# Layer-norm statistics taken one stage earlier, output stored in pieces, and query lengths by column tiles, in a 12-stage decoder kernel

## The reference

```python
def _layernorm(x, axis=-1, eps=1e-05):
    m = jnp.mean(x, axis=axis, keepdims=True)
    v = jnp.var(x, axis=axis, keepdims=True)
    return (x - m) / jnp.sqrt(v + eps)
...
# layer 1, cross-attention, for each of 16 heads with D = 128
q = rmsnorm(q, gq); k = rmsnorm(k, gk)      # x * rsqrt(mean(x^2) + eps) * g
```

## Time and profile before

| | |
|---|---|
| median of three runs | 1930.0 us (1928.4 to 1930.96) |
| profiled execution | 1931.94 us, its span 1930.2 us |
| busy, share of the span | PE 1709.8 us (89%), DVE 1174.4 (61%), ACT 927.5 (48%), POOL 442.2 (23%) |
| weight loads of PE | 1334.9 us (69%) |
| mean granted TensorE clock | 0.951 of full speed |
| DMA | 77.87 MB, 40 GB/s over the span |
| one row load of 129 KB (`xnT<-rows_sent`, 23 of them) | 2.0 us from issue to landing (median) |

### The profile page before, as it was taken

One profiled execution on the slowest core, in us unless ns is written; L12 is line 12 of the kernel. 1 busy time (PEld: TensorE's weight loads), 2 busy tenths in 40 slices (PEclk: granted clock), 3 DMA queues, 4 the chain that ended last, 5 costly groups with the idle time before them and its releaser, 6 DMA issues. The chain is left out here.

```text
span 1930.2 us, 37486 instructions
## 1 busy us (share of the span) xinstructions
PE 1709.8 (89%) x13958; PEld 1334.9 (69%) x13958; DVE 1174.4 (61%) x2339; ACT 927.5 (48%) x1966; POOL 442.2 (23%) x497
## 2 busy tenths in 40 slices
PE   7978846789999889977878879999999988999898
PEld 4767724569999745643667747777777776888666
DVE  3676687655555612226654577888888865666632
ACT  2445565245555511112254356766666744555532
POOL 1020011033333032221300133545454531000200
PEclk9999977899999989998979889999999999999999
DMA  2020001200010182221000100101010103110000
GB/s 100 3 90 3 4 29 50 93 17 26 25 29 28 53 326 42 45 52 43 14 2 3 42 9 26 33 25 33 25 33 25 33 9 127 36 33 24 1 1 23
DMA packets 27105, 77.87 MB, mean 40 GB/s; under 512 B 2928, under 2 KB 14832, under 8 KB 24560
## 3 DMA queue, kind: packets, MB, share of 16 engines
q1 hardware_dynamic: 22912, 71.17, 10.9%
q0 software_dynamic: 4080, 5.13, 1.7%
HBM read 63.01 MB, written 13.28 MB: 40 GB/s over the span
## 5 line engine op out<-in xcount | busy, mean ns | idle before, releaser
L2473 DVE SCALAR_TENSOR_TENSOR arena<-bank,arena 128x508 f32<-128x508 f32 (+2 forms) x204 | 151.6, 743 | 29.9 <-ACT arena L2469 17.9
L217 PE MATMUL bank<-const 128*128 128x256 f32 (+1 forms) x228 | 95.8, 535 | 33.7 <-PEq L65 33.7
L2599 PE MATMUL bank<-L3a_wo,L3a_y_gated 128*128 128x256 f32 x512 | 124.0, 386 | 0.0
L2827 DVE TENSOR_TENSOR L3a_decays<-L3a_decays,L3a_cb_masked 128x512 f32<-128x512 f32 x128 | 95.0, 804 | 43.9 <-ACT L3a_decays L2711 43.9
L2711 ACT ACTIVATE L3a_decays<-bank 128x512 f32<-128x512 f32 x128 | 66.1, 604 | 98.2 <-PE bank L2573 98.2
L2626 PE MATMUL bank<-L3a_xnT_high,L3a_w_high 128*128 128x512 f32 x256 | 106.3, 415 | 1.5 <-ACT L3a_decays L2711 1.5
L2599 PEld LDWEIGHTS bank<-L3a_wo,L3a_y_gated 128*128 128x128 f32 x512 | 92.4, 190 | 17.6 <-issue 7.3
L2626 PE MATMUL bank<-L3a_xnT_high,L3a_w_low 128*128 128x512 f32 x256 | 100.5, 393 | 0.0
L2626 PE MATMUL bank<-L3a_xnT_low,L3a_w_high 128*128 128x512 f32 x256 | 100.4, 392 | 0.0
L1885 PE MATMUL bank<-L1f_experts,xnT 128*128 x184 | 84.5, 602 | 1.0 <-DVE xnT L1987 0.7
L2922 POOL TENSOR_TENSOR arena<-arena 128x1024 f32<-128x1024 f32 x32 | 81.1, 2533 | 14.8 <-ACT arena L2718 14.8
(11 more groups left out here) (593 smaller groups left out, 4706.1 us busy)
## 6 DMA issues: line engine op xcount, KB each, us to landing
arena<-in_L3p SPq DMA_DIRECT2D x32, 388.0 KB, 3.0
L1f_experts<-in_L1f SPq DMA_DIRECT2D x8, 1536.0 KB, 19.3
arena<-in_L1x SPq DMA_DIRECT2D x18, 384.0 KB, 3.1
arena<-in_L3x SPq DMA_DIRECT2D x18, 384.0 KB, 3.0
arena<-in_L0f SPq DMA_DIRECT2D x1, 4224.0 KB, 13.6
arena<-in_L3f SPq DMA_DIRECT2D x1, 4055.0 KB, 12.6
rows_sent<-L1a_blank SPq DMA_DIRECT2D x1, 2967.0 KB, 13.9
xnT<-rows_sent SPq DMA_DIRECT2D x23, 129.0 KB, 2.0
```

The lines of the kernel that those rows point to most:

```text
L217: self.nc.tensor.matmul(self.k.ps[bank][:, 0:width], self.k.ident, self.k.const[:, 0:width], start=True, stop=True)
L2473: return nc.vector.scalar_tensor_tensor(dst[:, :, d:], psum[:, :, 0:P - d], wcol, dst[:, :, d:], ALU.mult, ALU.add)
L2599: mm = nc.tensor.matmul(ps[g // 2][:, (g % 2) * C:(g % 2 + 1) * C], yg[:, o, g * P:(g + 1) * P], wo[:, o, :], start=False, stop=False, ski ...
L2827: nc.vector.tensor_tensor(d, d, cbm[:, 4 * half:4 * half + 4, :].rearrange("p b t -> p (b t)"), ALU.mult).then_inc(S["dec_ready"], 1)
```

## The change

- `Norm(measured=True)`, in 11 of the 12 stages (not L0a): no `bn_stats`. DVE runs eight `bn_aggr`, ACT one square root for all eight batches, DVE one reciprocal and one bias. PE keeps the two opening unread matmuls, and has one more ahead of batches 1 and 2 only, not ahead of 3, 5, 6, 7.
- `measure` runs `bn_stats` in the stage before, on DVE behind each addition, after a wait for that addition's own semaphore. In L0f and L1a batches 0 to 5 are measured ahead of the last but one addition, in L3a all eight behind the last addition. L1f fetches x with two DMAs of 512 KB, and measures four batches behind each.
- `WideHeads.add` waits for each half of the last projection instead of for the whole.
- ACT preloads the table of the square root at the end of each stage from L0a to L3x.
- The output is stored from L3f by four DMAs of 256 KB, each behind its addition. "end" only clears semaphores.
- L1x: the lengths of a head come from four matmuls with ones (128x32) as weights and 256 squared columns moving, each to its own 32 partitions of bank 7; they stand ahead of the scores. DVE copies the 128x256 result to SBUF, PE transposes it in two pieces behind the scores, and DVE picks 8 columns of that.

```diff
+        if self.measured:
+            for b in range(NB):
                 nc.vector.bn_aggr(k.ln_mv[:, b, :], k.ln_stats[:, b, :]).then_inc(self.s_mv, 1)
+            self.scales(dve, 0)
+            for b in self.BY_DVE:
+                normed(b)
...
-                if j and self.busy:
+                if self.busy and b in ((1, 2) if self.measured else (1, 2, 3, 5, 6, 7)):
                     self.idle(pe, 1, C)
...
+def measure(k, dve, sem, added, batches):
+    dve.wait_ge(sem, added)
+    for b in batches:
+        k.nc.vector.bn_stats(k.ln_stats[:, b, :], k.x[:, b, :])
...
-    def add(self, dve):
+    def add(self, dve, N):
         x = self.k.x
         for n in range(4):
+            dve.wait_ge(self.s_y, 2 * N - 1 + n // 2)
             self.nc.vector.tensor_tensor(x[:, 2 * n:2 * n + 2, :], x[:, 2 * n:2 * n + 2, :],
-                                         self.k.ps[n][:, :].rearrange("p (b n) -> p b n", b=2), ALU.add)
+                                         self.k.ps[n][:, :].rearrange("p (b n) -> p b n", b=2),
+                                         ALU.add).then_inc(self.s_x, 1)
+            measure(self.k, dve, self.s_x, n + 1, (2 * n, 2 * n + 1))
...
+                nc.scalar.preload_act_table(ACT.Sqrt)
...
                 for n in (NB - 2, NB - 1):
+                    measure(k, dve, s_x, n, range(0, n) if n == NB - 2 else (n - 1,))
                     added(n)
+                measure(k, dve, s_x, NB, (NB - 1,))
...
                 sp.wait_ge(s_added, NT * 16)
-                sp.dma_start(x[:, :, :], k.sums[0:TOK, :].rearrange("(p b) c -> p b c", b=NB)).then_inc(s_fetched, 16)
-                sp.wait_ge(s_fetched, 16)
+                for n in range(2):
+                    bs = slice(4 * n, 4 * n + 4)
+                    sp.dma_start(x[:, bs, :], k.sums[0:TOK, :].rearrange("(p b) c -> p b c", b=NB)[:, bs, :]).then_inc(
+                        s_fetched[n], 16)
...
+                    measure(k, dve, S["x_added"], NB, range(NB))
...
+                        tr.free(pe, j, ("n", 0))
+                        pe.wait_ge(s_sq, j * 2 + 2)
+                        for r in range(4):
+                            mm = nc.tensor.matmul(tr.bank(("n", 0))[32 * r:32 * r + 32, 0:C], k.c["ones"][:, 0:32],
+                                                  sq[:, r * C:(r + 1) * C], start=True, stop=True)
+                        mm.then_inc(s_len, 1)
                     if back:
...
                         a.scores(pe, j, "", 1 - s)
                     if now:
-                        tr.free(pe, j, ("n", 0))
-                        pe.wait_ge(s_sq, j * 2 + 2)
-                        for b in range(NB):
-                            mm = nc.tensor.matmul(tr.bank(("n", 0))[:, b:b + 1], sq[:, b * P:(b + 1) * P],
-                                                  k.c["ones"][:, 0:1], start=True, stop=True)
+                        pe.wait_ge(s_lenc, j + 1)
+                        for n in range(2):
+                            mm = nc.tensor.transpose(tr.bank(("n", 0))[:, C + n * P:C + (n + 1) * P],
+                                                     lengths[:, n * P:(n + 1) * P], k.ident)
                         mm.then_inc(s_n, 1)
...
+                    if now:
+                        dve.wait_ge(s_len, j + 1)
+                        since(dve, s_n, j)
+                        nc.vector.tensor_copy(lengths[:, :], tr.bank(("n", 0))[:, 0:C]).then_inc(s_lenc, 1)
...
+                for n in range(4):
+                    sp.wait_ge(s_x, n + 1)
+                    sp.dma_start(k.out[:, 2 * n:2 * n + 2, :], x[:, 2 * n:2 * n + 2, :]).then_inc(s_out, 16)
+                sp.wait_ge(s_out, 64)
...
-                    sp.dma_start(out, k.x[:, :, :]).then_inc(s_out, 16)
                     for s in [*k.used, k.s_sent, k.s_added]:
                         sp.sem_clear(s)
-                    sp.wait_ge(s_out, 16)
-                    sp.sem_clear(s_out)
```

More of the change, by code:

```diff
@@ L123, with __init__ @@
     BY_ACT, BY_DVE = (0, 1, 2, 6), (3, 4, 5, 7)
-    def __init__(self, k, st, halves=None, turned=True, busy=True):
+    def __init__(self, k, st, halves=None, turned=True, busy=True, measured=True):
         self.k, self.nc, self.halves, self.turned, self.busy = k, k.nc, halves, turned, busy
+        self.measured = measured
         self.s_stats, self.s_mv, self.s_std = st.sem("ln_stats"), st.sem("ln_mean_var"), st.sem("ln_std")
@@ L199, in scalar @@
         for b in self.BY_ACT:
-            if b == 2:
+            if b == 2 and not self.measured:
                 std(1)
-            if b == 6:
+            if b == 6 and not self.measured:
                 act.wait_ge(self.s_nbias, 2)
@@ L599, in dve @@
             own = x[:, 2 * n:2 * n + 2, :].rearrange("p b n -> p (b n)")
-            self.nc.vector.tensor_tensor(own, own, self.k.ps[4 + n if self.turned else n][:, :], ALU.add)
+            self.nc.vector.tensor_tensor(own, own, self.k.ps[4 + n if self.turned else n][:, :],
+                                         ALU.add).then_inc(self.s_x, 1)
+            measure(self.k, dve, self.s_x, n + 1, (2 * n, 2 * n + 1))
 def clear(nc, t, sem):
@@ L1511, in _ @@
                         add(b - 2)
-                add(NB - 2)
-                add(NB - 1)
+                for b in (NB - 2, NB - 1):
+                    measure(k, dve, s_x, b, range(0, b) if b == NB - 2 else (b - 1,))
+                    add(b)
+                measure(k, dve, s_x, NB, (NB - 1,))
 def l1_xattn(k):
@@ L1552, in l1_xattn @@
         s_wh, s_qw = st.sem("w_high"), st.sem("q_w_ready")
+        s_len, s_lenc = st.sem("lengths_psum"), st.sem("lengths_copied")
         s_lns, s_rn = st.sem("log_ready"), st.sem("rnorm_ready")
@@ L2001, in _ @@
                                                 ALU.mult).then_inc(s_yc, 1)
+                for n in range(2):
+                    measure(k, dve, s_fetched[n], 16, range(4 * n, 4 * n + 4))
 def l2_attn(k):
@@ L3413, in program @@
     k = K()
-    k.nc, k.dram, k.parts, k.width = nc, dram, parts, width
+    k.nc, k.dram, k.parts, k.width, k.out = nc, dram, parts, width, out
     with ExitStack() as ctx:
```

90 lines of the change are left out of this document (55 added, 35 removed).

## The result

The changed kernel takes 1913.1 us (median of four, 1910.8 to 1915.5) against 1929.2 for the kernel before on the same chip: ratio 0.991, 95% interval 0.9893 to 0.9927, so 16 us faster by the medians and 17 by the ratio.

What follows compares the result with a forecast made beforehand. The openings were taken as one chain with PE bounding its later part, the L1x loop as PE's. Openings -23.1, moved statistics +13.9, clock +2.4, tail +1.0, L1x -14.3: -20.1 us, giving 1910 us, range 1903 to 1923.

Steps and rivals of the forecast that it cites:

- (c): Openings: transposes don't hold the clock, ten blocks start at half speed, 1.64 us each, 1926 us; chance 0.06.
- (d): L1x lengths: four column groups run one after another, +0.25 us a head, 1928 us, no change; chance 0.06.
- (e): L1x lengths: groups run one by one and each pass awaits its weight load, 1940 us; chance 0.05.
- The step from 3.32 to 2.1 for the first transpose: Full-clock openings: the earlier square root brings PE's first transpose to 2.1 us after the barrier instead of 3.32.
- The four unread matmuls at 1.76: Stage openings: removing four unread matmuls between transposes, 0.44 us each, shortens the chain by 1.76 us.
- The 1.1 for two close additions in L2x: L2x's end: two additions stand close together and the queue behind them is late, costing 1.1 us.
- the 1.75 forecast: L1f's fetch: x's second half lands one issue (0.32) later and four statistics follow, costing 1.75 us.
- None to four can fall, I take two: Clock in the four fast stages' openings: longer barrier gaps, 1.2 us per fall, 2.4 us taken (0 to 4.8).
- Each of the fast stages would lose 0.57: Openings: if the square root's table load stayed at the barrier, each full-clock stage would lose 0.57 us.
- Rival (b): Openings: the preload doesn't take away the table load at the stage's start, 2.3 us, 1912 us; chance 0.08.
- 1.06: L1x loop: PE saves 1.06 us a head with the new lengths; 14 heads less 0.5 make 14.3 us.
- Rival (a): L1x loop: not PE's alone, PE waits for q, half of the 14.3 us is kept, 1917 us; chance 0.15.

Runs made afterwards that it cites:

- experiment 8: The changed kernel without the preloads of the square root's table at the stages' ends; ratio to the kernel before 0.991.
- experiment 5: The changed kernel with the statistics back in every stage's opening, unread matmuls ahead of batches 1 and 2 only; ratio to the kernel before 0.9873.
- experiment 2: The changed kernel with L1x's eight length matmuls of before in place of the length tiles; ratio to the kernel before 0.9945.
- experiment 4: The changed kernel with the wait for the stored quarters moved behind the 44 semaphore clears; ratio to the kernel before 0.9894.
- experiment 7: The changed kernel without any unread matmul between transposes in the measured stages, the two opening ones kept; ratio to the kernel before 0.9894.
- 9: The changed kernel once more, unaltered (the repeat); ratio to the kernel before 0.9907.
- experiment 10: The changed kernel with all six unread matmuls between the transposes put back; ratio to the kernel before 0.9984.
- experiment 1: The kernel before with only the L1x length tiles of the change; ratio to the kernel before 0.9943.
- experiment 3: The kernel before without the unread matmuls ahead of batches 3, 5, 6, 7, statistics left in place; ratio to the kernel before 0.9919.
- 6: The changed kernel with statistics moved for L0f only, stores awaited behind clears shared by four engines; ratio to the kernel before 0.9879.
- 11: The changed kernel with statistics moved for L0f only and clears shared by four engines, timed again; 1904.3 us, ratio to the kernel before 0.9854.

## Why the prediction was right, and where it wasn't

**The time.** 1910 was forecast, 1913.1 measured. The forecast mechanism held in nearly every place, and rivals (c), (d), (e) are refuted by the traces. Two terms were mis-sized, L1x by 5 us and the other blocks, which I had at nothing, by 3 the other way. That the second made up for more than half of the first is luck: it hangs on where the clock stood in these two profiles.

**Openings.** The step from 3.32 to 2.1 for the first transpose: 2.21. The four unread matmuls at 1.76: 1.74. So 2.9 in L2f and L3a: 2.91 and 2.92, with the block at 5.77 after the barrier (5.7 was said). L1a, L1f and L2a at 1.76: 1.72, 1.74, 1.74. L0f 1.7: 1.92. L3x 0.9: 1.22. In L2x it was 2.49, since ACT's first normed batch started 1.2 after the start of the square root and not 0.78, as in L2f; I had 0.75 to 0.91 for all. L3f gave only 0.73: I counted it with the stages at half clock whose opening stays as long as it was, but its clock came back among the transposes, later after the barrier than before, so that the transposes ran at half clock too. In L1x 1.9 was forecast; 0.52 is in this profile and 2.22 in the repeat, as the clock fell or held. But in the repeat it fell 0.9 us into the block, which took 255.1 us instead of 252.8, so that most of the 2.22 was lost again there.

**Ends of stages.** 0.78 was said for L0a, L0x, L2a and L2f: 0.78, 0.80, 0.79 in L0a, L0x and L2f. The 1.1 for two close additions in L2x is wrong: it has 0.79. L2a has 1.12 in its place, but for another reason: its additions are 1.73 apart, and DVE waits 0.97 at that barrier where it waits 0.64 elsewhere, so DVE isn't what the barrier waits for. In experiment 8, without preloads, L2a's end is 0.34 shorter; in experiment 5, with the preload and without the moved statistics, it is 1.27, as before. So the preload has a part in it, how stays open. L0f and L1a 0.5: 0.44, 0.45. L1x and L3x 2.0: 1.74 and 1.69. L3a 2.9: 2.74, the long row of this timeline (DVE):

```profile
1566.16 3.23 DVE L2948 SCALAR_TENSOR_TENSOR x<-bank,L3a_rms,x 128x256 f32<-128x256 f32 x8
1569.42 2.71 DVE L264 BATCH_NORM_STATS2 ln_stats<-x 128x6 f32<-128x256 f32 x8
```

In L1f from the fetch to the barrier 7.1 us pass instead of 5.5, so 1.6 for the 1.75 forecast, but not as I had it. The rows of the changed kernel:

```profile
854.11 0.79 SPq L1867 DMA_DIRECT2D x<-rows_added  x2
```

```profile
857.96 2.72 DVE L264 BATCH_NORM_STATS2 ln_stats<-x 128x6 f32<-128x256 f32 x8 [9.24 <-DMA x<-rows_added]
```

The first half lands 3.85 after the issue, earlier than I assumed, and the second before the first's statistics are through; all eight `bn_stats` are exposed in one row, none hides under the second half. The wrong mechanism came out at the right size, which is luck.

**The clock.** "None to four can fall, I take two": one of the four (L0x) fell in this profile. Over the seven profiles with moved statistics (after, 2, 4, 7, 8, 9, 10) L0x, L2x, L2f and L3a make 28 openings, of which 15 fell, 2.1 in each. Over the six with their statistics at home (before, 1, 3, 5, 6, 11) none of 24 fell. What differs is PE's idle time at the barrier, 2.15 us there (2.5 in L2x) and 1.36 here. Neither the unread matmuls nor the preload make the difference: openings fell in experiment 10 with all of the first and in experiment 8 without the second. L1x, L1f and L3f, whose clock was at 1.00 before the barrier in every profile too, give further gaps:

| PE's idle time at the barrier | where | fell by 1.6 us behind the barrier |
|---|---|---|
| 1.1 | L1x, statistics at home | 0 of 6 |
| 1.4 | L0x, L2x, L2f, L3a, at home | 0 of 24 |
| 1.55 | L1x, moved | 3 of 7 |
| 2.0 | L1f, L3f in 5, 6, 11 | 3 of 6 |
| 2.15 to 2.5 | L0x, L2x, L2f, L3a, moved | 15 of 28 |
| 3.15 | L1f, L3f in before, 1, 3 | 6 of 6 |
| 4.8 to 4.9 | L1f, L3f, moved | 14 of 14 |

So the longer the gap, the more of them fall. No run lengthens the gap and nothing else, so that the gap is the cause is what all these rows say, but isn't isolated. A fall costs 1.3 in an opening (7.09 instead of 5.77).

**Transposes and the clock.** Rival (c) is refuted by experiment 7: the clock rises among transposes, and all nine blocks behind openings without unread matmuls between the transposes start at 1.00. What the Trainium skill, TensorE: Matmul & The Clock Gate, Part 4, states, that transposes don't count as PE being busy for the clock, isn't borne out by these rows (128x128, fp32).

**Preload.** "Each of the fast stages would lose 0.57": the square root comes 0.58 later without it. That nothing moves at half clock is right. Rival (b) didn't come true, and would have been smaller than its 2.3 us, for the falls of the clock hide it.

**The tail.** Landing 2.3 after the issue: 2.3. 1.0 longer: 1.04. SP's clears were late next, as experiment 4 shows.

**L1x.** Here the size failed, in three terms. Four groups with 256 columns take 0.57 and not 0.43; with the transposes 0.71 and not 0.65, and the head is shortened by 0.89 to 0.92, not 1.06. Only 13 distances shrink, not 14: the last one has no lengths in it, and PE waits there for the probabilities, as before. And the first two heads, which I had at no gain and 0.5 of cost, lose 1.3: the transposes wait 0.54 for DVE's copy in the first pass, and PE's wait for q ahead of L1626 grows from 0.82 to 1.22 us in the second. That gives -10.3, which experiment 1 measured. The rest to the -9.3 of the profile is the clock in the last pass (timeline of PE):

```profile
636.20 0.82 PE L752 MATMUL bank<-const,L1x_p 128*128 128x128 f32 x4 [1.48 <-DVE L1x_p L815]
636.82 3.48 PE L762 MATMUL bank<-L1x_pT,L1x_ctx_rows 128*128 128x128 f32 x16
```

The same 16 records took 2.03 us before. This distance is 14.0 to 14.1 in the changed kernel (both profiles) and in experiment 8, 12.6 in experiments 1, 4, 5, 6, 7, 10 and 11. Rival (a) had half of the gain lost to a wait for q; there is no such wait in the loop beyond the 0.33 of before.

**What I didn't draw from my own numbers.** The sum was right and its split was there. Of the 23.1 us for the openings, 14.1 were eight times the unread matmuls' 1.76, which need no moved statistics: my own count of the normed batches, done at some 5.4, puts them before the last transposes want them (experiment 3: right in L2f, wrong in L0x). What the move itself buys was about 7 (four times 1.16, L0f's 1.7, L3x's 0.9) against 13.9 and 2.4 of price. A sum over parts that are put in together hides that one of them loses. Experiments 5 and 10 show it: some 6 to 9 us, 7.6 by the traces.

**The other blocks.** I had them at nothing. They differ from profile to profile without any change in their code, by where the clock stands. The largest are L1a, 2.5 longer, and L3a, 2.5 shorter. L1a's block takes 57.1 to 57.4 us to its last matmul in before and in experiments 1, 2, 4, 6, 9 and 10, and 59.6 to 59.8 in after and in 3, 5, 7, 8 and 11. The clock is at 0.50 for 10 to 14 us of it in the first group and for 17 in the second. One part of it, at half clock in after, and in experiment 2, where the clock comes back within it (0.74 in the mean):

```profile
370.81 3.06 PE L1453 MATMUL bank<-L1a_gw,L1a_productT 128*128 128x256 f32 x6
```

```profile
371.33 2.20 PE L1453 MATMUL bank<-L1a_gw,L1a_productT 128*128 128x256 f32 x6
```

Why the clock comes back earlier in one execution than in another I didn't test.

## What to carry to other kernels

Price each part of a joined change against the version that has all the other parts, not against the kernel before; a part that loses can ride on one that wins. Work moved from behind a barrier to ahead of it is only worth it where it fills a wait that is there: the last addition of a stage is on the path as much as the next opening, and L0f, where the opening was bound by DVE and ACT alone, was the one place where it clearly paid by the trace. Where PE idles at a barrier, a longer gap can cost its clock, so a shorter opening and a longer gap have to be summed together; and small housekeeping such as semaphore clears has a cover that is lost when the transfer above it is moved.

## What was not expected of the hardware

- Adding 0.8 us to PE's idle time at a barrier (1.36 to 2.15) went with a fall of the granted clock in 15 of 28 openings, against 0 of 24; gaps of 3.15 and more had it in 20 of 20.
- The clock's return isn't repeatable: in the same code it moves the block of L1a by 2.5 us from one execution to the next, which is more than most of the single terms of this change.
- Four column groups of 32 with 256 fp32 columns each take 0.57 us for 8 records, 0.071 a record. An unread fp32 matmul that moves 256 columns with all 128 columns of weights takes 0.22 a record (0.44 for the two from 1050.87 to 1051.31 above), so four groups together are 3.1 times as fast, not four times. The projection's 0.117 for 256 columns is no measure for this: its operands are of another type, `fp32r`, and its calls are one record each and not two.
- Semaphore clears cost SP 0.057 us each. GpSimd and VectorE take longer for one (instructions of 0.044 and 0.054 us where SP's are 0.028), yet eleven of them on each at the same time are done within 0.8 us.
- Two DMAs of 512 KB issued one behind the other had the first half ready 3.85 us after the issue and the second no more than 1.4 us later, since the fifth of the eight `bn_stats` didn't wait.

The row of the changed kernel that shows the type of the projection's operands:

```profile
504.77 0.41 DVE L1768 TENSOR_TENSOR L1x_product_low<-bank,L1x_product_high 128x256 fp32r<-128x256 f32 x1
```
